# A four-layer residual chain on one core: output projection behind the turned x1, the adapters' first product in front of layer 3, attention in front of scores, x1 kept in memory

## What is computed

```python
x = x + (x @ W.T + scal[a] * (x @ A[a].T) @ Bm[a].T)      # layer 0: W and a low-rank adapter (rank 16) per sequence
x = x + einsum('bct,bcd->bdt', x, w1[s])                   # layer 1: 64x64 matrix per sequence, over the tokens
x = x + attention(x)                                       # layer 2: causal, 16 heads of 32, q scaled per sequence
x = x + einsum('bct,bcd->bdt', x, w3[u])                   # layer 3: as layer 1, with another table
```

## Time and profile before

| | us |
|---|---|
| median of three runs | 637.3 (637.06 to 637.41) |
| the profiled execution's own time | 637.91 |
| its span, first to last instruction | 636.2 |
| TensorE busy with matmuls | 620.0 (97%) |
| VectorE busy | 386.3 (61%) |
| ScalarE busy | 209.6 (33%) |
| GpSimd busy | 140.9 (22%) |
| DMA | 31.48 MB, 49 GB/s over the span |

### The profile page before, as it was taken

The page is one execution under the profiler, slowest core; times in us unless marked ns, Lnnn a source line. Parts: engine busy times, 40 slices in busy tenths (PEclk is TensorE's granted clock), DMA queues, the critical chain, the costliest instruction groups (busy, mean ns, idle before and its releaser), DMA issues.

```text
span 636.2 us, 19724 instructions
## 1 busy us (share of the span) xinstructions
PE 620.0 (97%) x7814; PEld 525.5 (83%) x7814; DVE 386.3 (61%) x546; ACT 209.6 (33%) x404; POOL 140.9 (22%) x118
## 2 busy tenths in 40 slices
PE   6999999999999999999999999999999999999998
PEld 5797878879788787988879798887988879798885
DVE  4667666556567565666656567565656755556464
ACT  4444233322233332233323223332223323223222
POOL 2005040320403113040310404022040311304031
PEclk9999999999999999999999999999999999999999
DMA  7621103012030110202011020211203011010101
GB/s 268 183 90 26 43 1 90 12 34 63 4 90 7 58 41 18 77 4 91 8 58 41 8 86 5 70 29 24 72 3 91 8 58 43 15 51 2 40 1 67
DMA packets 41111, 31.48 MB, mean 49 GB/s; under 512 B 15547, under 2 KB 30907, under 8 KB 41083
## 3 DMA queue, kind: packets, MB, share of 16 engines
q1 hardware_dynamic: 37130, 25.06, 13.6%
q10 hardware_dynamic: 3952, 6.03, 2.9%
HBM read 22.15 MB, written 8.91 MB: 49 GB/s over the span
## 4 chain that ended last, share of the span: by engine, by line
PE 94%; DVE 2%; issue 1%; DMA 1%; ACT 1%; POOL 0%; ACTq 0%; DVEq 0%
PE banks L548 10%; PE banks L553 10%; PE banks L549 10%; PE banks L599 5%; PE banks L574 5%; PE banks L641 5%; PE banks L648 5%; PE banks L642 5%; PE banks L525 5%; PE banks L500 4%; PE banks L578 4%; PE banks L498 4%; PE banks L576 4%; PE banks L502 4%; PE banks L591 4%; PE banks L615 3%
## 5 line engine op out<-in xcount | busy, mean ns | idle before, releaser
L1220 POOL TENSOR_TENSOR probs<-probs,row_max 128x1024 f32<-128x1024 f32 x32 | 61.0, 1906 | 319.4 <-DVE row_max L1041 319.4
L548 PE MATMUL banks<-x1T_hi,w_hi 128*128 128x256 f32 x512 | 130.5, 287 | 0.0
L549 PE MATMUL banks<-x1T_hi,w_lo 128*128 128x256 f32 x512 | 128.1, 283 | 0.3 <-issue 0.3
L548 PEld LDWEIGHTS banks<-x1T_hi,w_hi 128*128 128x128 f32 x512 | 98.0, 191 | 1.9 <-issue 0.4
L549 PEld LDWEIGHTS banks<-x1T_hi,w_lo 128*128 128x128 f32 x512 | 98.1, 192 | 0.0
L553 PE MATMUL banks<-x1T_lo,w_hi 128*128 128x256 f32 x512 | 82.5, 283 | 1.0 <-issue 1.0
L553 PEld LDWEIGHTS banks<-x1T_lo,w_hi 128*128 128x128 f32 x512 | 70.6, 192 | 1.2 <-issue 1.2
L1027 DVE TENSOR_TENSOR qkT<-banks,beta 128x512 f32<-128x512 f32 x32 | 22.1, 691 | 61.0 <-PE banks L553 61.0
L1045 DVE TENSOR_REDUCE row_sum<-probs 128x16 f32<-128x1024 f32 x32 | 39.0, 1220 | 25.7 <-ACT probs L860 25.7
L574 PE MATMUL banks<-w_hi,x1T_hi 128*128 128x512 f32 x128 | 51.7, 404 | 1.8 <-issue 1.2
L963 DVE COPY x<-banks 128x512 f32<-128x512 f32 x16 | 11.1, 691 | 69.2 <-PE banks L517 69.1
(11 more groups left out here) (130 smaller groups left out, 1047.8 us busy)
## 6 DMA issues: line engine op xcount, KB each, us to landing
x_in<-in_x_dram SPq DMA_DIRECT2D x60, 128.0 KB, 2.4
out_dram<-x_y SPq DMA_DIRECT2D x15, 512.0 KB, 2.8
b_sel<-b_parts SPq DMA_DIRECT2D x180, 32.0 KB, 1.7
w_in<-in_L_cond_weights_dram SPq DMA_DIRECT2D x128, 16.0 KB
probsT<-in_L_cond_W_dram ACTq DMA_DIRECT2D x1, 1024.0 KB, 6.9
probs<-in_L_cond_Wk_dram ACTq DMA_DIRECT2D x1, 1024.0 KB, 6.3
qkT<-in_L_cond_Wq_dram ACTq DMA_DIRECT2D x1, 1024.0 KB, 7.6
probsT<-in_L_cond_Wv_dram ACTq DMA_DIRECT2D x1, 1024.0 KB, 7.1
```

Of the source, the lines that this page charges most:

```text
L548: nc.tensor.matmul(out_ap, w_hi[:, w, c, cols], x1T_hi[:, c, :], start=(c == 0), stop=False)
L549: nc.tensor.matmul(out_ap, w_lo[:, w, c, cols], x1T_hi[:, c, :], start=False, stop=False)
```

## The change

- TensorE's order of a middle step becomes: values, layer 0, first probabilities, layer 1, second probabilities, x1, output projection of i-1, the adapters' first product of i+2 (the last of its eight products behind the wait for x2), layer 3 of i-1, keys, queries, attention, scores. Step 0 has no output projection and no layer 3, step 14 no adapters' product; the last step keeps its order.
- Attention is written to banks 1 and 3 (`AT`), the adapters' first product to bank 3 (`DOWN`).
- GpSimd's copy of x1 is removed. SyncE stores x1 to memory (`store_x1`) and loads it into `x1_kept` (`load_x1_rows`) once the additions of the pair before are done.
- ScalarE makes both high parts of attention; VectorE makes only the two low parts, behind the queries' scaling. The lists of ScalarE, VectorE, GpSimd and SyncE are put in the order of TensorE's.
- `pT_copied(i, HG)`, the wait for the second probabilities' copies, stands before the last part of the queries and no longer before the last piece of x1.

```diff
-X1T, Q = SC[0:2], (OUT[0], MIX[0])
+X1T, Q, AT = SC[0:2], (OUT[0], MIX[0]), (OUT[1], MIX[1])
...
-DOWN = OUT[1]
+DOWN = MIX[1]
...
+    def store_x1(i):
+        sp.wait_ge(x1_copied_act, i + 1)
+        sp.wait_ge(x1_copied_dve, i + 1)
+        sp.dma_start(one_pair(x1_rows, i), x1[:]).then_inc(x1_stored, 16)
+    def load_x1_rows(i):
+        if after(i, -1):
+            sp.wait_ge(x2_added, TILES * i)
+        else:
+            sp.wait_ge(x1_stored, 16)
+        sp.dma_start(x1_kept[:], one_pair(x1_rows, i)).then_inc(x1_kept_loaded, 16)
...
     def step(i):
         if after(i, 2):
             gather_own_b(i + 2)
+        if after(i, 1):
+            store_x1(i + 1)
+        if after(i, 3):
+            gather_w1(i + 3)
+        load_x1_rows(i)
+        if after(i, 3):
+            turned_in(i + 3)
         if after(i, -1):
             store_y(i - 1)
-        if after(i, 3):
-            turned_in(i + 3)
         if after(i, 1):
             at3 = pair_indices(idx3_row, w3.shape[0], i + 1)
             sp.wait_ge(w3_ready, i + 1)
-            gather(w3_in, w3, at3, w3_loaded, True)
-        if after(i, 3):
-            gather_w1(i + 3)
+            gather(w3_in, w3, at3, w3_loaded, True, range(PSEQ - 1))
+            sp.wait_ge(x1_stored, 16 * (i + 2))
+            gather(w3_in, w3, at3, w3_loaded, True, range(PSEQ - 1, PSEQ))
...
+    def adapters_down(i, x2_of=None):
...
+                if x2_of is not None and (c, t) == (NC - 1, TILES - 1):
+                    layer3_ready(x2_of)
...
             last.then_inc(q_mm, 1)
     def values(i):
-        if after(i, -1):
-            pe.wait_ge(attn_split, SEQT * i)
-        for t in range(TILES):
-            if t == 1 and after(i, 1):
-                pe.wait_ge(xa_summed, i + 1)
+        for t in range(TILES):
...
     def step(i):
         prev, nxt, nxt2 = after(i, -1), after(i, 1), after(i, 2)
         values(i)
-        if prev:
-            for t in range(TILES):
-                layer2_out(i - 1, t)
-        if nxt:
-            layer0(i + 1)
-        if prev and nxt:
-            layer3_ready(i - 1)
+        if not nxt:
+            last_step(i)
+            return
+        layer0(i + 1)
         pe.wait_ge(probs_done[0], i + 1)
         turn_probs(i, 0, range(7))
-        if nxt:
-            layer1_ready(i + 1)
+        layer1_ready(i + 1)
         turn_probs(i, 0, range(7, 8))
-        if nxt:
-            if prev:
-                layer3(i - 1)
-            layer1()
+        layer1()
         pe.wait_ge(probs_done[1], i + 1)
-        turn_probs(i, 1, range(7))
-        if not nxt:
-            layer3_ready(i - 1)
-        turn_probs(i, 1, range(7, 8))
-        if not nxt:
-            layer3(i - 1)
-            pT_copied(i, HG)
-            attend_last()
-            return
+        turn_probs(i, 1, range(8))
         pT_copied(i, 1)
         pe.wait_ge(x1_copied_act, i + 2)
         turn_x1(i + 1, 0, range(NC))
         pe.wait_ge(x1_copied_dve, i + 2)
-        turn_x1(i + 1, 1, range(NC - 1))
+        turn_x1(i + 1, 1, range(NC))
+        if prev:
+            for t in range(TILES):
+                layer2_out(i - 1, t)
+        if nxt2:
+            adapters_down(i + 2, x2_of=i - 1 if prev else None)
+        elif prev:
+            layer3_ready(i - 1)
+        if prev:
+            layer3(i - 1)
+        pe.wait_ge(x1_hi_done, TILES * (i + 2))
+        for m in range(NC):
+            if m == 2 and nxt2:
+                pe.wait_ge(xa_summed, i + 2)
+            key_part(i + 1, m)
+            if not prev and m > 1:
+                if m == 2:
+                    pT_copied(0, HG)
+                turn_part(WO, m - 2)
         if prev:
             pe.wait_ge(y_copied_act, i)
-            pe.wait_ge(y_copied_dve, i)
         else:
             pe.wait_ge(v_copied, TILES)
-        pT_copied(i, HG)
-        turn_x1(i + 1, 1, range(NC - 1, NC))
-        attend()
-        pe.wait_ge(x1_hi_done, TILES * (i + 2))
-        for m in range(NC):
-            key_part(i + 1, m)
-            if not prev and m > 1:
-                turn_part(WO, m - 2)
-        pe.wait_ge(attn_split, SEQT * (i + 1))
         for m in range(NC):
             if m == 2:
                 pe.wait_ge(k_copied_act, i + 2)
+            if m == 3:
+                pe.wait_ge(k_copied_dve, i + 2)
+                pT_copied(i, HG)
+                if prev:
+                    pe.wait_ge(y_copied_dve, i)
             query_part(m)
             if not prev and m < 2:
                 turn_part(WO, m + 2)
-        if nxt2:
-            adapters_down(i + 2)
+        attend()
         if not prev:
             pe.wait_ge(turned_lo, GROUPS_OF[WO][-1] + 1)
         scores(i + 1)
...
-        if nxt:
-            x0_copy(i + 1)
+        if not nxt:
+            last_step(i)
+            return
+        x0_copy(i + 1)
         copy_pT(i, 0)
-        if not nxt:
-            copy_pT(i, 1)
+        x1_copy(i + 1)
+        copy_pT(i, 1)
+        x1T_hi_part(i + 1)
+        if nxt2:
+            x_hi(i + 2)
         if prev:
             copy_y(i - 1)
-        if nxt:
-            x1_copy(i + 1)
-            copy_pT(i, 1)
-        if nxt:
-            x1T_hi_part(i + 1)
-        if not nxt:
-            for t in range(TILES):
-                act.wait_ge(av_mm, i + t + 1)
-                copy(last_attn(attnT_hi[:], t, 0), last_attn_bank(t, 0)).then_inc(attn_hi_done_act, 1)
-            return
+        if nxt2:
+            xa_low_part(i + 2)
+            xa_hi_part(i + 2)
+        if not prev:
+            take_hi(GROUPS_OF[WO][0], w_hi[:, WO, 0, :])
+        copy_k(i + 1)
+        if not prev:
+            for c in range(1, NC):
+                take_hi(GROUPS_OF[WO][c], w_hi[:, WO, c, :])
         act.wait_ge(av_mm, i + 1)
-        copy(attn_of(attnT_hi[:], 0), attn_bank(0)).then_inc(attn_hi_done_act, 1)
-        if nxt2:
-            x_hi(i + 2)
-        if nxt:
-            if not prev:
-                take_hi(GROUPS_OF[WO][0], w_hi[:, WO, 0, :])
-            copy_k(i + 1)
-            if not prev:
-                for c in range(1, NC):
-                    take_hi(GROUPS_OF[WO][c], w_hi[:, WO, c, :])
-            if nxt2:
-                xa_low_part(i + 2)
-                xa_hi_part(i + 2)
+        for r in range(SEQT):
+            copy(attn_of(attnT_hi[:], r), attn_bank(r)).then_inc(attn_hi_done, 1)
...
+        if not nxt:
+            last_step(i)
+            return
+        x0_copy(i + 1)
+        copy_pT(i, 0)
+        x1_copy(i + 1)
+        copy_pT(i, 1)
+        x1T_lo_part(i + 1)
+        if nxt2:
+            turn_x(i + 2)
         if prev:
             for t in range(TILES):
                 add_x1(i - 1, t)
-        if nxt:
-            x0_copy(i + 1)
-        copy_pT(i, 0)
-        if not nxt:
-            copy_pT(i, 1)
+        if nxt2:
+            sum_xa(i + 2)
+            scale_xa(i + 2)
         if prev:
             copy_y(i - 1)
-        if nxt:
-            x1_copy(i + 1)
-            copy_pT(i, 1)
-        if nxt:
-            x1T_lo_part(i + 1)
-        if not nxt:
-            for t in range(TILES):
-                dve.wait_ge(av_mm, i + t + 1)
-                copy(last_attn(attnT_hi[:], t, 1), last_attn_bank(t, 1)).then_inc(attn_hi_done_dve, 1)
-                for r, done in enumerate((attn_hi_done_act, attn_hi_done_dve)):
-                    dve.wait_ge(done, i + t + 1)
-                    rest(last_attn(attnT_lo[:], t, r), last_attn_bank(t, r),
-                         last_attn(attnT_hi[:], t, r)).then_inc(attn_split, 1)
-            return
-        dve.wait_ge(av_mm, i + 1)
-        copy(attn_of(attnT_hi[:], 1), attn_bank(1)).then_inc(attn_hi_done_dve, 1)
-        for r, done in enumerate((attn_hi_done_act, attn_hi_done_dve)):
-            dve.wait_ge(done, i + 1)
+        if nxt2:
+            xa_lo_part(i + 2)
+            x_lo(i + 2)
+        if not prev:
+            for c in range(2):
+                take_lo(GROUPS_OF[WO][c], w_lo[:, WO, c, :], w_hi[:, WO, c, :])
+        copy_k(i + 1)
+        if not prev:
+            for c in range(2, NC):
+                take_lo(GROUPS_OF[WO][c], w_lo[:, WO, c, :], w_hi[:, WO, c, :])
+        scale_q(i + 1)
+        for r in range(SEQT):
+            dve.wait_ge(attn_hi_done, SEQT * i + r + 1)
             rest(attn_of(attnT_lo[:], r), attn_bank(r), attn_of(attnT_hi[:], r)).then_inc(attn_split, 1)
...
-    def keep_x1(i):
-        if after(i, -1):
-            pool.wait_ge(x2_added, TILES * i)
-        pool.wait_ge(x1_copied_act, i + 1)
-        pool.wait_ge(x1_copied_dve, i + 1)
-        nc.gpsimd.tensor_tensor(x1_kept, x1, zero[:].unsqueeze(2).to_broadcast([P, TILES, D]), ALU.add)\
-            .then_inc(x1_kept_done, 1)
     def step(i):
         for g in range(HG):
             pool.wait_ge(s_max, HG * i + g + 1)
             with_rows(ALU.subtract, g, row_max, s_less_max)
         pool.wait_ge(inv_done, HG * i + 1)
         with_rows(ALU.mult, 0, row_inv, probs_done[0])
-        keep_x1(i)
```

(78 more changed lines are left out.)

28 lines of the change are left out of this document (5 added, 23 removed).

## The result

The changed kernel takes 657.15 us (median of 4 runs, 654.20 to 659.63) against 637.18 (636.47 to 637.41) for the kernel before in the same session: a ratio of 1.0308 (1.0291 to 1.0325). The forecast was 645.0 with a range up to 648.5. Sign and mechanism of a middle step are right, the time is not: it came out slower by 20 us instead of 7.7.

A forecast was written before the change was run, and what follows sets the result against it. TensorE's instruction order and the short waits between them were taken to bound the kernel. Middle steps +4.7, step 14 +0.65 and step 0 +2.4 sum to +7.7: 645.0 us from a median of 637.3, range 639.5 to 648.5.

The forecast's parts named there:

- Moved: attention between queries and scores: Middle step: attention moves between queries and scores, projection stands alone; one more change between matmul kinds, +0.06, no wait.
- The clock falls in step 0: Rival: step 0's new hole halves TensorE's clock for keys and queries, costing 1.8 to 3.5, 647 to 648.5; chance 0.10.
- Middle step: Steps 1 to 13: sum of removed wait, added wait and kind change, +0.36 each, bounds +0.10 to +0.46; times 13, +4.7.
- Removed: the wait before x1's last piece: Middle step: probabilities' copy is needed only before the queries' last quarter, so x1 costs 0.93 instead of 1.28, -0.35.
- Added: a wait for x2: Middle step: adapters' last product waits for x1's addition to the output projection, delaying layer 3; +0.65, bounds 0.45 to 0.70.
- Kinds: Middle step: eleven instead of ten changes between kinds of matmul, +0.06, bounds 0 and 0.11.
- Step 0: First step: x's turning delays the adapters' product, +3.6; less 0.77 and 0.5 from old holes; +2.4, bounds +1.6 to +2.9.
- Step 14: No adapters' product covers the wait for the addition: +1.0 less 0.35 gives +0.65, bounds 0.4 and 0.8.
- Softmax: Middle step: first result ready 9.6 after values start, wanted at 11.5; hidden. Rival that it or the queue is late: 0.05.
- the adapters' sum: Middle step: copies and sum behind layer 3 finish by E+4.8 (E: projection's end), keys' third quarter needs them at E+5.0; hidden.
- covers the addition: Rival: adapters' product hides the addition, so layer 3 does not wait in 13 middle steps; -1.4, 635.9; chance 0.10.
- No difference: Rival: addition partly covered, its wait costing 0.15 instead of 0.65 per middle step; together +0.9, 638.2; chance 0.08.

The follow-up runs named there:

- e8_after_both: Changed kernel with layer 3 behind the first quarter of the keys and step 0's adapters' product behind the keys; 647.75 us, ratio 1.0165.
- e1_attend_before_q2: Changed kernel with attention in the middle of the queries, between queries 1 and 2; 653.93 us, ratio 1.0256.
- e5_step0: Changed kernel with the adapters' product of step 0 alone placed behind the keys, in another bank; 652.71 us, ratio 1.0251.
- e7_before_reordered: Kernel before the change, both halves of the probabilities turned in one go, layers 1 and 3 behind them, keys and attention swapping banks; 627.67 us, ratio 0.9854.
- e3_layer3_after_key0: Changed kernel with layer 3 and its wait for x2 behind the first quarter of the keys; 651.07 us, ratio 1.0198.
- e4_no_memory_trip: Changed kernel without x1's stores and loads for all pairs but the first, all adding pair 0's x1; 655.37 us, ratio 1.0300.

## Why the prediction was wrong

**The step that failed** is "*Moved: attention between queries and scores*". It was priced at 0.06 a step, one change between kinds of matmul, with the words "there is no wait in either". These words are about engines that TensorE might wait for, and as such they held. But what the move put together, 128 products of attention and 128 of scores with as many weight loads, 512 short instructions in about 3 us, was never looked at as a stream, and was priced from a middle step alone. In steps 1, 13 and 14 that stream breaks off for 1.5 to 2.1 us. Three holes cost 6.4 us and the clock behind them 4.4: 10.8 of the 14.0 us (21.7 - 7.7) by which the forecast fell short in the profiled execution. The rest is 2.2 in the three terms that it had and 1.0 ahead of step 0. Shown: the holes in the scores of these three steps go when large matmuls stand between attention and scores (two kernels, and a third with all edits), and stay when the wait for x2 is gone, when step 0 is mended, and when x1 does not travel. Shown too: with all else mended they are what is left, 10.4 us in `e8_after_both`.

**What makes the holes** is not shown by an experiment, but the traces point one way. Step 1 is the first pass of the loop, and steps 13 and 14 are written out behind it; passes 2 to 12 run the same instructions as pass 1 and have no hole in any scores (1.52 to 1.76). The DMA queues of the changed kernel, from 130 to 545 us and from 545 to 640:

```profile
## 3 DMA queue, kind: packets, MB, share of 16 engines
q1 hardware_dynamic: 32208, 28.85, 25.6%
...
q1 hardware_dynamic: 2656, 3.67, 11.6%
q8 instruction: 8, 0.13, 0.5%
q14 instruction: 4, 0.03, 0.1%
```

In the stretch of the repeated passes not one instruction packet moves; where code runs for the first time they do (8 of 16 KB in q8). A single one started 0.8, 0.6 and 0.3 before the holes of steps 1, 13 and 14, none in the holes, and TensorE went on 2.3 to 2.7 after its start (for which engine it was the profile does not say). Counted from the end of the packet the distance is nearly constant: the packets end at 121.34, 585.73 and 628.06, and the weight loads resume at 122.80, 587.19 and 629.56, 1.5 us later each time.

The same holds in the other kernels. From step 0 on, the ten traces have 28 holes of 0.6 us or more (none in `e1_attend_before_q2`) in the weight loads of values, keys, queries and scores that no engine releases and that the repeated passes do not have; each ends 1.2 to 1.6 us after the end of a 16 KB packet of q8. Two of them are in the kernel before: the 1.23 in the keys of step 0, which no row explained (1.4 after a packet's end), and 0.63 in the values of step 1. So the holes are not new. The change made them longer where it put the small products together.

So TensorE seems to have used up its instructions faster than the next block arrived. Step 0 of the changed kernel has the 256 small products on their first pass too, and no hole (scores 1.52); it has the wait of 3.8 in front, and in `e5_step0`, without this wait, a hole of 1.1 appears in its scores, as was expected there from a fetch that no longer gets time to run ahead. The Trainium skill (Runtime: NRT & Kernel Launch, Instruction fetch mechanics) says that the sequencer fetches the next 16 KB block while it executes the current one, and that this is mostly hidden; the packets agree, and the holes are a place where it is not hidden. No run here changed the fetch itself, for instance by moving the stream against the blocks, so that the fetch is the cause rests on these times.

**The clock.** The rival "*The clock falls in step 0*" was right in kind: behind the hole of 3.79 the granted clock fell to 0.5 and 0.6 and made keys and queries 1.7 longer (3.4 us at half pace); it had a chance of 0.10, and named one place of four. Its range, 647 to 648.5, missed because it knew one hole only. A granted clock of 0.5 after step 0 was also among the forecast's own signs of being wrong. The rule of the Trainium skill weighed there (TensorE: Matmul & The Clock Gate, the HAM clock gate) agrees in kind with what followed this hole: the clock halved behind idleness and given back while TensorE worked.

**Middle step.** Forecast +0.36, measured +0.48. *Removed: the wait before x1's last piece*: -0.35 foretold, -0.49 measured (1.28 to 0.79); right, and the 0.14 more is probably the change of kind, which now falls on the projection behind. *Added: a wait for x2*: +0.65 foretold, +0.68 measured (0.57 to 1.25). Kinds: +0.06 foretold; the projection takes 5.76 instead of 5.59 and layers 1 and 3, now apart, 2.04 instead of 1.88, +0.33. With the 0.14 taken off that is 0.19, above the bound of 0.11. The forecast took the two layers as 0.9 each; together they took 1.88, apart each takes 1.02. Times 13: 6.2, just above the upper end of 6.0. That the sum is nearer to the forecast than its terms is because two of them err in opposite directions.

**Step 0 and step 14.** Step 0 was foretold at +2.4 and measured +2.8. The wait for x's transpose, 3.79 in the weight loads, costs 3.5 from start to start (from the first piece of x1 to the next group 1.13 before, 4.64 now; 3.6 foretold). The multiplication no longer slows the turning (2.04 to 1.27, -0.77 as foretold); keys and queries took 14.89 instead of 14.72, since the clock took 1.7 where the old hole gave some 1.5 back (0.5 foretold). That +2.8 lies near the +2.4 is luck: without the clock it would have been +1.1, under the lower bound of 1.6. Step 14: +0.65 foretold, +0.9 measured without hole and clock, just above its bound of 0.8.

**Covers that held.** Softmax, the adapters' sum, GpSimd's copy and the two DMAs cost nothing: no middle step shows another wait, and taking the memory trip out gave 1.8 us of the median, less than the spread of either kernel's runs (5.4 and 4.9). The rivals "*covers the addition*" and "*No difference*" fall with the hole of 0.31 and the +0.68.

## What to carry to other kernels

Where code runs for the first time, short instructions are cheapest when they are spread between long ones. Before putting two groups of a hundred small matmuls together, look at these steps (the first pass of a loop, what is written out behind it), not at one in the middle, and price a hole there with the half clock behind it. In the repeated passes the neighbourhood cost nothing here, and pulling the groups apart cost 0.4 to 0.5 a step. A wait is taken away where it stands, as in `e7_before_reordered`, by giving it another group to hide behind; moving three large pieces around it costs a new wait, more changes of kind and a new neighbourhood for every piece. And a period taken from one middle step times the number of steps needs its counterpart, a look at the first and last steps by themselves.

## What the hardware showed unexpectedly

- TensorE stopped for 1.1 to 2.1 us in the middle of 128 equal products with no engine to wait for, only on code's first pass, where 256 small products stand in a row. A quarter of a projection between them takes this down to 0.3 or less in steps 1, 13 and 14. Shorter stops of the same kind, 0.6 to 1.3 in the weight loads, also occur among large products, mostly in the values of step 1. All of them end 1.2 to 1.6 us after a 16 KB instruction packet has landed.
- The granted clock fell to half behind holes of only 1.5 to 2.1 us, each fall costing 1.2 to 1.6 us of the values. It is not certain to fall: in the profiled executions it did so behind three holes of three in the changed kernel, in `e3_layer3_after_key0` and in `e8_after_both`, and behind none of three of 1.4 to 2.1 us in `e4_no_memory_trip` and `e5_step0` (in other executions of these two it did, by their mean clock of 0.990 and 0.992). That is also the spread of the changed kernel's runs: mean granted clock 0.989 at 659.63 and 658.95, 0.994 at 655.35, 0.997 at 654.20. In the two kernels with attention apart and step 0's hole left in, the clock was 0.997 and the spread 1.3 and 2.5.
- In the middle of the loop scores cost as much behind attention as behind the adapters' product of the kernel before (1.72 to 1.76), and 1.89 to 1.94 directly behind the large products of the queries. Whether the change of kind or the scaling of the queries costs the difference, no run separates.
